# A fused attention and gated feed-forward kernel: row maxima in one fused VectorE pass, eleven gate/up units, one run of values a group, PSUM banks by table, and an own order for each engine

## The reference

```python
xn = _layernorm(x, axis=-1)
q, k, v = (xn @ W.T for W in (Wq, Wk, Wv))          # 16 heads of 16
att = einsum(q, k) / sqrt(16) + triu(neg)           # causal
s = (softmax(att) @ v) @ Wo.T
gate = _silu(_qlinear(xn, wq_gate, s_gate))         # 704 hidden columns; weights are integers,
up = _qlinear(xn, wq_up, s_up)                      # W = (wq - 128) * scale
g = _silu(_qlinear(gate * up, wq_down, s_down))
return x + s * g
```

## Time and profile before

| | |
|---|---|
| time, median of 3 runs | 328.07 us |
| span of the profiled execution, first to last instruction | 323.8 us |
| TensorE matmuls busy | 297.4 us (92%), 2352 records |
| VectorE busy | 184.7 us (57%) |
| ScalarE busy | 173.6 us (54%) |
| GpSimd busy | 142.4 us (44%) |
| mean granted TensorE clock | 0.983 |

### The profile page before, as it was taken

One profiled execution on the slowest core, in us unless ns is written; L12 is line 12 of the kernel. 1 busy time (PEld: TensorE's weight loads), 2 busy tenths in 40 slices (PEclk: granted clock), 3 DMA queues, 4 the chain that ended last, 5 costly groups with the idle time before them and its releaser, 6 DMA issues.

```text
span 323.8 us, 6058 instructions
## 1 busy us (share of the span) xinstructions
PE 297.4 (92%) x2352; PEld 206.7 (64%) x2352; DVE 184.7 (57%) x309; ACT 173.6 (54%) x251; POOL 142.4 (44%) x240
## 2 busy tenths in 40 slices
PE   0697689999999999999999999999999999999984
PEld 0575457667767567687767557687857566687443
DVE  5773873657455557766356557655356657743433
ACT  3546237654366587534366687534366666533840
POOL 5068763511147565221257565221264475223461
PEclk9999797999999999999999999999999999999997
DMA  7948792023858204032778120032768120001202
GB/s 279 275 138 200 195 145 67 5 69 127 173 90 156 43 3 130 15 122 72 177 147 169 29 68 2 18 120 66 180 141 172 27 69 3 2 2 67 69 0 67
DMA packets 21008, 31.56 MB, mean 97 GB/s; under 512 B 2148, under 2 KB 9956, under 8 KB 20980
## 3 DMA queue, kind: packets, MB, share of 16 engines
q1 hardware_dynamic: 20528, 30.50, 39.1%
q10 hardware_dynamic: 452, 0.67, 0.6%
HBM read 20.32 MB, written 10.49 MB: 95 GB/s over the span
## 4 chain that ended last, share of the span: by engine, by line
PE 67%; DMA 12%; SPq 5%; POOL 5%; issue 3%; DVE 3%; ACT 3%; ACTq 0%; POOLq 0%
PE ps L430 14%; PE ps L432 11%; PE ps L431 11%; PE ps L600 9%; PE ps L581 8%; DMA kp<-qk_scratch 7%; PE ps L540 7%; DMA sdb<-in_sd 4%; PE ps L552 4%; PE ps L608 2%; SPq L368 2%; POOL zbuf L901 1%; SPq L377 1%; SPq L370 1%; POOL hid L911 1%
## 5 line engine op out<-in xcount | busy, mean ns | idle before, releaser
L806 ACT ACTIVATE pt<-ps 128x1024 f32<-128x1024 f32 x80 | 81.8, 1027 | 36.0 <-PE ps L581 35.9
L949 POOL TENSOR_SCALAR_AFFINE_SELECT pt<-pt 128x256 f32<-128x256 f32 (+1 forms) x112 | 47.5, 439 | 94.8 <-ACT pt L806 94.1
L911 POOL TENSOR_TENSOR hid<-hid 128x512 f32<-128x512 f32 x24 | 31.3, 1302 | 55.9 <-ACT hid L748 36.2
L1080 DVE TENSOR_REDUCE mx<-ps 128x2 f32<-128x1024 f32 x32 | 39.1, 1224 | 20.2 <-PE ps L552 19.5
L540 PE MATMUL ps<-kp,qp 48*128 48x512 f32 (+3 forms) x256 | 36.2, 342 | 7.7 <-DVE mx L1080 3.1
L430 PE MATMUL ps<-xh,guh 128*128 128x512 f32 x96 | 42.2, 439 | 0.5 <-DVE u L1061 0.5
L600 PE MATMUL ps<-pt,vt 128*17 128x256 f32 (+3 forms) x512 | 42.2, 436 | 0.0
L581 PE MATMUL ps<-qp,kp 50*128 50x512 f32 (+3 forms) x256 | 39.6, 369 | 0.6 <-DMA qp<-ctr 0.3
L1085 DVE TENSOR_REDUCE mx<-ps 128x4 f32<-128x1024 f32 x16 | 19.6, 1226 | 35.0 <-PE ps L552 35.0
L1082 DVE TENSOR_REDUCE mx<-ps 128x2 f32<-128x768 f32 x32 | 30.6, 956 | 14.2 <-PE ps L552 14.1
L581 PEld LDWEIGHTS ps<-qp,kp 50*128 50x128 f32 x256 | 20.2, 184 | 28.8 <-issue 22.1
(11 more groups left out here) (117 smaller groups left out, 521.1 us busy)
## 6 DMA issues: line engine op xcount, KB each, us to landing
qk_scratch<-hid SPq DMA_DIRECT2D x24, 256.0 KB
qp<-qk_scratch SPq DMA_DIRECT2D x14, 256.0 KB, 4.6
kp<-qk_scratch SPq DMA_DIRECT2D x14, 256.0 KB, 6.4
qp<-qk_scratch SPq DMA_DIRECT2D x18, 128.0 KB, 4.3
kp<-qk_scratch SPq DMA_DIRECT2D x18, 128.0 KB, 6.7
xr<-in_x SPq DMA_DIRECT2D x4, 512.0 KB, 3.5
out<-xr SPq DMA_DIRECT2D x8, 256.0 KB, 3.9
xin<-in_x SPq DMA_DIRECT2D x3, 512.0 KB, 4.0
```

The costliest lines, as they stand in the source:

```text
L806: nc.scalar.activation(pt[:, 2 * kk:2 * kk + 2, :], ps[:, base:base + 2, :], ACT.Exp, scale=SCALE).then_inc(exp_done, 1)
L911: nc.gpsimd.tensor_tensor(a, a, hid[:, m % 2, 1, :], ALU.mult).then_inc(h_done, 1)
L949: mm = nc.gpsimd.affine_select(out=diag, in_=diag, compare_op=ALU.is_ge, fill=0.0, base=0, pattern=[[0, diag.shape[1]], [1, P]], channel_m ...
L1080: mm = nc.vector.tensor_reduce(mg[:, :, kk, 3], both, AX.X, ALU.max, negate=True)
```

## The change

- Row maxima. The four bf16 matmuls of an `m` unit are gone. VectorE runs one `tensor_tensor_reduce` per block of scores: it adds a bf16 mask from SBUF (`maskt`), takes the minimum of the negated sums into one column of `mx`, and writes the sums back over the PSUM bank. Each is two instructions in its list, one over the block and one that writes the 128x1 result. The work on a group is cut into the two banks of a unit (`maxa`, `maxb`).
- Gate/up. The last hidden tile has 64 columns only. Its gate and its up half share one unit, so a batch has 11 `gu` units instead of 12, and the low part of that tile's hidden values lies in the free half of `hh`, made by VectorE (`hidden_tail`), so the down projection has 17 matmuls a row tile instead of 18.
- Values. `pv` is one unit a group: sixteen matmuls in one run, with 32 weight columns a head (`vt` is padded with zeros). The last group is cut in two halves of the rows.
- PSUM. Any unit takes the banks that its entry in the table names; it waits for what held them last.
- Order. Each engine, SyncE too, has one list for the whole kernel. `pt` has 12 slots, `ctr` two, `c_loaded`, `pack_loaded` and `qk_stored` are split into more semaphores.
- Head. 34 matmuls on zeros come first on TensorE. The down weights are scaled by one VectorE instruction instead of two on GpSimd.
- Tail. The output projection of the last batch adds its two parts in PSUM, so two products and two sums fall away.

```diff
-    [("m", 0, 8), ("s", 0, 0), ("v", 0, 0)],
-    [("m", 0, 9), ("pv", -1, 10), ("pv", -1, 11), ("s", 0, 1)],
...
+TENSOR_ORDER = """
+t:0:0:0 t:0:1:1 qk:0:0:0 qk:0:1:1 qk:0:2:2 qk:0:3:3 gu:0:0:0 gu:0:1:1 gu:0:2:2 gu:0:3:0 gu:0:4:1 gu:0:5:0 v:0:0:2
+m:0:0:01 m:0:1:34 m:0:2:56 v:0:1:7 m:0:3:01 gu:0:6:2 m:0:4:37 gu:0:7:4 m:0:5:56 gu:0:8:2 m:0:6:04 gu:0:9:1 gu:0:10:3
...
+def place_banks():
+    held = {}
+    for kind, b, n, banks in TENSOR:
+        if banks:
+            BANKS[kind, b, n] = banks
+            BEFORE[kind, b, n] = [held[k] for k in banks if k in held]
+            for e, k in enumerate(banks):
+                held[k] = (kind, b, n, e)
...
             def maxima(b, m):
...
-                for r in range(2):
-                    for e in range(2):
-                        part = slice(64 * e, 64 * e + 64)
-                        bank = ps[:, base + e, :]
...
-                        mm = nc.tensor.matmul(dst, rows2[part, r, :], tri, start=False, stop=(r == 1))
                 mm.then_inc(sm_ready, 1)
...
-                    mm = nc.vector.tensor_reduce(mg[:, :, kk, 3], both, AX.X, ALU.max, negate=True)
...
+                bank = ps[:, BANKS["m", b, m][e], :]
+                for a, j, c in pair_blocks(kk, e):
+                    i = TT - 1 - j
+                    wide = (i + 1) * P
+                    part = bank[:, c:c + wide]
+                    mm = nc.vector.tensor_tensor_reduce(part, part, maskt[:, T - wide:], -1.0, TOP, ALU.add, ALU.min,
+                                                        mg[:, e, a // 2, i:i + 1])
+                mm.then_inc(max_done, 1)
...
             def down(b, n):
...
+                    for m in range(HF):
+                        split3(dst, hh[:, m, rows], hl[:, m, rows], wdh[:, m, :], wdl[:, m, :], m == 0, False)
+                    nc.tensor.matmul(dst, hh[:, HF, rows], wdh[:, HF, :], start=False, stop=False)
+                    mm = nc.tensor.matmul(dst, hh[:, HF, rows], wdl[:, HF, :], start=False, stop=True)
...
             def values(b, n):
...
+                for j in tiles:
+                    at = max(first, j * P)
+                    for a in range(GH):
+                        kk, e, c = SLOT_OF[a, j]
+                        mm = nc.tensor.matmul(ps[32 * a:32 * a + VC, bank, at:end], vt[:, j, GH * g + a, :],
+                                              pair(b, 5 * g + kk)[:, e, c + at - j * P:c + end - j * P],
+                                              start=(j == 0), stop=(j == tiles[-1]))
...
+            pe.wait_ge(cn_zero, 1)
+            for _ in range(WARM):
+                nc.tensor.matmul(ps[:, 7, 0:P], cn[:], cn[:], start=True, stop=True)
```

More of the change, by code:

```diff
@@ L157 @@
-HEAD_DONE |= {("c", 0, 0), ("ccp", 0, 0)} | {(k, b, i) for k in ("bn", "mom", "root", "xn") for b in range(2) for i in range(TT)}
-def entries(engine, steps, b, s):
-    first = FIRST[engine].get(s, []) if b == 0 else []
-    last = LAST[engine].get(s, []) if b == B - 1 else []
-    todo = [(kind, b + o, n) for kind, o, n in steps[s] if 0 <= b + o < B]
-    return [x for x in todo if x not in HEAD_DONE] + [(kind, b + o, n) for kind, o, n in first + last]
-def tail_units():
-    return [(kind, B - 1 + o, n) for kind, o, n in TAIL]
@@ new lines, with units @@
+"""
+def units(text):
+    out = []
+    for word in text.split():
+        kind, b, n, *banks = word.split(":")
+        out.append((kind, int(b), int(n), tuple(int(c) for c in banks[0]) if banks else ()))
+    return out
+TENSOR, SCALAR, VECTOR, GPSIMD, SYNC = map(units, (TENSOR_ORDER, SCALAR_ORDER, VECTOR_ORDER, GPSIMD_ORDER, SYNC_ORDER))
+BANKS = {}
+BEFORE = {}
+def place_banks():
[6 more added lines that the diff above has]
+                held[k] = (kind, b, n, e)
@@ L182, in pair_blocks, with bank_of @@
+place_banks()
+for last_n in range(2):
+    BANKS["o", B - 1, last_n] = BANKS["oa", B - 1, last_n]
+def bank_of(kind, b, n):
+    return BANKS[kind, b, n][0]
 def pair_blocks(kk, e):
@@ L428, in _ @@
         def _(pe):
+            w = Waits(pe)
             def split3(dst, lh, ll, rh, rl, start, stop):
@@ new lines, in _ @@
+            pe.wait_ge(cn_zero, 1)
+            for _ in range(WARM):
+                nc.tensor.matmul(ps[:, 7, 0:P], cn[:], cn[:], start=True, stop=True)
+            pe.wait_ge(ident_done, 1)
+            work = {"t": transpose_x, "qk": project_qk, "v": project_v, "gu": gate_up, "dn": down, "m": maxima,
+                    "c": transpose_c, "s": scores, "pv": values, "zt": transpose_z, "z2": transpose_back,
+                    "o": out_unit, "oa": project_out_first}
+            for kind, b, n, _ in TENSOR:
+                work[kind](b, n)
@@ L1071, in maxima @@
+            def maxima(b, m, e):
                 g, kk = divmod(m, 5)
@@ L1232, in _ @@
-            work = {"max": maxima, "xlo": split_x, "qlo": chunk_lo, "gate": gate, "u": gate_f, "norm": norm_z, "zlo": z_lo,
-                    "fin": finish, "oa": finish_first, "bn": statistics, "mom": moments}
-            for b in range(B):
-                for s in range(STEPS):
-                    for kind, of, n in entries("vector", VECTOR_STEPS, b, s):
-                        work[kind](of, n)
-            for kind, of, n in tail_units():
-                unit(kind, of, n)
+                nc.vector.tensor_tensor(part, u[:, n, :], part, ALU.add).then_inc(last_out_done, 1)
@@ L1243 @@
+            for kind, b, n, _ in VECTOR:
+                work[kind](b, n)
 def kernel(**inputs):
```

1283 lines of the change are left out of this document (545 added, 738 removed), and 18 rows, old and new, of the table TENSOR_STEPS.

## The result

The changed kernel is slower: 336.27 us median of 4 runs (335.26 to 337.89) against 327.65 us (325.46 to 328.97) for the kernel before on the same chip, a ratio of 1.030 (1.024 to 1.037). The forecast was 296.6 us and its range ended at 313. The profiled execution took 337.07 us, 335.2 of them span.

What follows compares the result with a forecast made beforehand. TensorE's own work was taken as the bound: 323.8 us of span - 28.0 work + 2.0 waits - 4.0 head - 1.5 tail = 292.3, plus 4.3 around it gives 296.6 us; 8-in-10 range 286 to 313.

Steps and rivals of the forecast that it cites:

- TensorE's work: On TensorE, masks, gate/up, down, splits and values together: -28.0 us, all in work taken to be the bound.
- `m` units with their masks: On TensorE, the mask matmuls of 32 narrow and 48 wide units go: -14.9 us.
- 512-column matmuls: On TensorE, gate/up: 4 units of 6 matmuls at 0.23 us fall away, -5.5 us.
- 256-column ones: On TensorE, down projection: one matmul less in 16 row tiles at 0.12 us, -1.9 us.
- the splits: TensorE's array changes its split 165 times instead of 202: taken as -6 us, between 4.4 and 7.4.
- VectorE: Fused maxima and other new work raise VectorE from 184.7 to about 224 us (218 to 263), still below TensorE.
- Rival 1: On VectorE, the fused operation runs at half speed: 333 us, slower than before; chance 0.07.
- Waits: In the middle, shared banks and slower VectorE make TensorE wait: +2.0 us, between nothing and 15.
- Head: Kernel start: warm matmuls and a clear GpSimd queue against a later first store: -4.0 us, bounds -7 to +5.
- Rival 2: Bank and queue waits in the middle, with VectorE at its upper end: 308 us (303 to 318); chance 0.17.
- Rival 4: The orders give the saved work back whole: within 0.5% of 328 us; chance 0.03.
- Values: On TensorE, 8 more matmuls for the split last group: +0.3 us.

Runs made afterwards that it cites:

- one_run: The kernel before with each group's values in one run of 16 matmuls, at the third part's place, and seven pairs of weight slots for five: 353.25 us, ratio 1.081.
- filled: The changed kernel with 80 more matmuls whose results nobody reads, placed in TensorE's list ahead of seven units that stood waiting: 337.36 us, ratio 1.028.
- instant_store: The changed kernel without the query/key stores of the second to fourth batch; their pack loads read the first batch's chunks: 306.21 us, ratio 0.941.
- both: The changed kernel with a separate staging buffer for query/key chunks and SyncE's stores and a maxima row ahead of bulk loads: 333.32 us, ratio 1.021.
- own_no_wait: The changed kernel with full stores, a separate staging buffer, and pack loads reading the first batch's chunks without waiting for later stores: 329.67 us, ratio 1.010.
- own_rows_no_wait: The changed kernel with full stores, a separate staging buffer, pack loads not waiting for later stores, and bias rows issued by ScalarE: 335.64 us, ratio 1.022.

## Why the prediction was wrong, point by point

**TensorE's work** came out right in sum, -29.7 us for -28.0, and only in part for the reasons given. By kind: `m` units with their masks -12.6 (predicted -14.9; -14.2 with the fused pass alone), 512-column matmuls -7.0 (-5.5), 256-column ones -3.4 (-1.9), values -2.4 (+0.3), `s` units -4.0 (no term), the rest -0.3. The -6 for the splits has no row of its own: values and `s` units together may hold it, -6.4 for -5.7, but `one_run` had 30 changes of the split fewer and only 0.7 us less work. So that term is not shown.

**VectorE** was right in kind and a little high: 208.7 us for 224, since the read of the accumulator costs 0.02 to 0.05 us and not 0.10. Rival 1, a fused pass at half speed, is out: a 512-element record has 0.713 us. The Trainium skill, VectorE: DVE Perf Modes, section The DRAIN you can't avoid, would have put it at the upper end by the rule that the prediction names; the same section adds that a next operation that is not held starts earlier. The rows here are on that side, since passes of 512 start 0.62 us apart with records of 0.71.

**Waits** is the step that failed: "I take +2.0, near today's value, since each engine has its own order and `m` units run ahead of their `s` units by about as much as before". Between 60 and 300 us it was 22.2 us of idle time for 1.7, and 12.5 us lost to a clock that had been full: 33.0 us more, and I had allowed 15. The bound had one mechanism in it, a bank that VectorE gives back late. The runs put in its place the exchange of q and k: with a sixteenth of the stores' bytes the same window has 7.3 us idle and 5.3 lost. I had priced that transfer only in the head. The number of bytes did not change, nor did the pack loads' time to land by much; what changed is that TensorE has 30 us less work to put over them, that SyncE issues half of the stores behind 2 MB of loads (packs and `x`), and that more waits in other lists end on them. Which of these three weighs most stays open: giving SyncE the old sequence for the stores alone gained nothing, and the kernel before was not run without its stores. Its middle has 1.7 us of idle time at full clock, so they cost it next to nothing there.

**The clock** was no term at all. It was at full level through the middle before, and I left it there, although a stop of 7.4 us is followed by 5 us at 0.55. In the changed kernel the lower clock costs 19.3 us and comes with the stops: with a sixteenth of the stores' bytes it costs 10.2. `filled` gained 4.3 us up to 86 us by keeping it up, and the next stop took all but 1.0 of that. How much of the 19.3 us is a cost of its own stays open.

**Head**, predicted -4. By 60 us TensorE had done 38.6 us of real work before and 31.5 now: +7.1, beyond my bound of +5. The first `m` unit came at 31.9, earlier than my 33 to 37, so the delay that I had worked out was not it: the output weights landed at 15.1 us, not at 19.3, and the first store was issued at 18.8, not at 23.6. The time went at 44.2, 5.7 us for the second part of the first pack loads, and at 56.7 for rows, and the lower clock after each. The warm matmuls brought little: the eight transpositions took 1.04 us instead of 1.94, but started at 10.42 instead of 9.71, since the warm ones ran over. The head is as slow in the versions without later stores: `instant_store` has 32.3 us of real work by 60 us, which makes 10.3 of the 11.8 us by which its span misses 292.3.

**Rivals.** Rival 2 was the right family (waits in the middle) with the wrong engine and a third of the size. Rival 1 was nearest in time, 333 us, by luck, since its mechanism is out. Rival 4, that the orders give the saving back whole, is the next. It got 3%, because "the middle has no slack to hide it". That sentence was the fault: in a middle without idle time the waits of other engines can be hidden by the work, and taking work away can uncover them.

**Values**, +0.3: TensorE's work on them fell by 2.4 us, but the edit forces the order. In the old one, at the place of the third part, it costs 27 us.

The account of the span: work -1.7 against the forecast, middle +31.0, head +11.1, the rest (behind 300 us) +2.5, together 42.9 us between 292.3 and 335.2. The 4.3 us that I put around the span were too many: the profiled execution has 1.9.

## What to carry to other kernels

When a kernel is full on one engine, list what that engine's work covers, transfers above all, with the time from the first chunk's store to the unit that reads it back, before counting a saving of work as a saving of time. A transfer that was hardly waited for can come to cost 28 us when the work over it shrinks by a tenth and the order around it changes; which of the two did it here was not told apart. To find such a cost, shrink its bytes and keep its waits: taking one wait away at a time gave 1 and 4 us here, both together 7, the bytes 28. And try the parts of a large change alone: the fused pass without the rest won 2.5%, and the run of values without the rest lost 8%. The gate/up part alone was not run.

## What the runs showed of the hardware

- The fused pass (two inputs, one PSUM and one bf16, written back to PSUM, with a running minimum) runs at about the rate of the others. From start to start it takes 0.62 us for 512 elements and 0.52 for 384 in the changed kernel. The prediction's 0.60 and 0.47, worked out from other operations, leave 0.02 to 0.05 us for the instruction that reads its accumulator.
- In or behind stops of 5.7, 1.9, 7.4 and 4.0 us TensorE's granted clock fell to its lower level for 6.8 us each (from 42.1, 55.7, 96.7 and 154.7 us in the changed kernel), behind one of 1.7 for 10.2 us (from 182.0), and in `both` for up to 17.1 us.
- In `own_no_wait` TensorE got an 8 KB transfer 12.1 us after its issue (89.98 to 102.12), with 4 MB issued ahead of it since 74.2. In `own_rows_no_wait`, where ScalarE issued them, two such transfers issued from 147.58 released TensorE at 158.19.
